# Score maxima turned earlier, norms by a power on GpSimd, one g maximum a slot, in a fused cross-attention and ternary feed-forward block

## The chip, the cores and the metric

The kernel runs on one core of a Trainium2 chip. The metric is the device time of one execution in microseconds; less is better. Times of the kernel before were taken in three runs.

## The reference

The input x is 64 batches of 64 rows of 256, the context is 64 batches of 64 rows of 64. One attention layer with 16 heads and one quantised feed-forward layer are applied, each with a residual.

```python
def attention(hidden_q, kv_c, Wq, w_kc_q, w_kc_kv, W_qr, W_kr, Wo):
    q_big = einsum('bshk,hkq->bshq', (hidden_q @ Wq.T).reshape(b, s, H, K), w_kc_q)
    kv_rope = kv_c * cos + rotate_half(kv_c) * sin
    q_r = einsum('bshq,hqr->bhsr', q_big, W_qr)
    k_r = einsum('bld,hdr->bhlr', kv_rope, W_kr)
    attn = softmax(einsum('bhsr,bhlr->bhsl', q_r, k_r), axis=-1)
    ctx_c = einsum('bhsl,bld->bhsd', attn, kv_rope)
    return einsum('bhsd,hkd->bshk', ctx_c, w_kc_kv).reshape(b, s, H * K) @ Wo.T

def bitlinear158(x, w):
    xn = x / maximum(norm(x), 1e-12) * sqrt(d)
    scale = 127 / clip(max(abs(xn)), 1e-5)          # one scale a row
    xq = clip(round(xn * scale), -128, 127) / scale
    wq = clip(round(w / clip(mean(abs(w)), 1e-5)), -1, 1) * clip(mean(abs(w)), 1e-5)
    return xq @ wq.T

x = x + attention(layernorm(x), ctx, ...)
x = x + bitlinear158(gelu(bitlinear158(layernorm(x), w1)), w2)   # 256 -> 1024 -> 256
```

## The kernel before

The 4096 rows of x make 32 tiles (`NT`) of 128 rows, each two batches. The weights of the attention are folded first: `ah`, `al` (high and low part) take a normed x straight to the queries against the rotated context, `bh`, `bl` take the contexts straight to the output. Each such product is three matmuls in f32r (high by high, low by high, high by low). The first 36 us load and fold; then comes one loop `for n in range(LAST)`, written out in the same form for every engine, that is, five instruction streams which meet only at counting semaphores. An iteration is called **slot n** here. In slot n the engines work on different tiles at once:

- TensorE (PE), in order: `scores(n)`; in even slots `up(n-7)` in both halves (first feed-forward product, bf16); `queries(k, b)`; in odd slots `x_t` (transposes of the next normed x); `project(n-3, 0)` (first half of the output product, 12 matmuls); `turned(n)`, one transpose of `red`, which holds the score maxima of tile n and the exponent sums of tile n-1; `project(n-3, 1)`; `queries(k, b+1)`; in odd slots `up(n-7, 0)`; `shifts(n)` (subtracts the maxima from the scores, in PSUM); `contexts(n-1)`; `down(n-10)` (second feed-forward product); in odd slots `up(n-7, 1)`.
- VectorE (DVE): `quadrant_max(n)` from the scores; `x_max(n-4)`; in even slots `norms`; `row_max(n)` and `row_sum(n-1)` from the transposed `red`; `divide(n-2)` (contexts by the sums); in odd slots `x_lo`; `residual(n-3)`; in odd slots `x_scale`; in even slots `g_max` of two tiles, `g_scale` and `finish` (output with its scale); `quadrant_sum(n)` after the exponential; up to slot 13 the `statistics` of the layer norm of two tiles at the slot's end.
- ScalarE (ACT): gelu, copies out of PSUM, squares, exponentials. Gelu and exponential need different tables, loaded each time (1.28 us).
- GpSimd (POOL): in even slots 4 to 14 `reciprocal_deviations` (four small steps with one power); `x_round`, `g_round` (quantisation, two passes each), `ctx_lo` (low part of the contexts), `centre`, `norm_x`; early on the ternary weights.
- The queue of SP: the transposing transfers `turn_x` (of `xq`) and `turn_g` (of `qb`), `shift_rows(n)` (the row maxima spread over `shift`, which `shifts(n)` reads), `rinv_rows`/`rinv_spread` (reciprocal sums through DRAM to `rb`), `store`.

`norms(j)` makes `scl`, the scales of two x tiles and two g tiles together: a floor, a reciprocal square root by a bit trick and three Newton steps (`rsqrt`, L189 to L201), a product with the maximum and a last floor and factor; 14 instructions of 128x4 elements, each of which waits for the one before. Its semaphore is `norm_steps`; gelu and `finish` wait for it.

`QB` is a pair of PSUM banks that serve queries, transposed x, and `up` in turn (`USES` fixes the order; a use waits until the use two before it has been copied out). So `up(n-7, 0)` of an odd slot waits for `xt_lo` (DVE `x_lo`), and `queries(k, b)` of an even slot waits for the first gelu of that slot. The other bank names: `SB` scores, `CB` contexts, `T` transposed `red`, `O` projection and second product.

Of the kernel before, what the change touches and what calls it, by code (L numbers as in the profile page):

```python
# [24 lines left out]
P = 128  # L25
# [4 lines left out]
F = 1024  # L30
# [16 lines left out]
NEWTON = 3  # L47
RSQRT_OPS = 3 * NEWTON + 2
# [6 lines left out]
NORM_STEPS = RSQRT_OPS + 3  # L55


def build(nc, x, kv, wq, wk_t, wqr, wkr_t, wkv, wo_t, w1_t, w2_t, consts, out):
    with ExitStack() as ctx:
# [32 lines left out]
        least, wfactor = [sb(n, [P, 4], F32) for n in ("least", "wfactor")]  # L92
# [96 lines left out]
        def rsqrt(e, v, y, t, done, n):  # L189

            def step(ins):
                nonlocal n
                n = n + 1
                ins.then_inc(done, 1)
                e.wait_ge(done, n)
            step(e.tensor_scalar(t.bitcast(I32), v.bitcast(I32), 1, None, ALU.arith_shift_right))
            step(e.tensor_scalar(y.bitcast(I32), t.bitcast(I32), -1.0, float(0x5F3759DF), ALU.mult, ALU.add))
            for _ in range(NEWTON):
                step(e.scalar_tensor_tensor(out=t, in0=y, scalar=-0.5, in1=y, op0=ALU.mult, op1=ALU.mult))
                step(e.scalar_tensor_tensor(out=t, in0=t, scalar=1.0, in1=v, op0=ALU.mult, op1=ALU.mult))  # L200
                step(e.scalar_tensor_tensor(out=y, in0=t, scalar=1.5, in1=y, op0=ALU.add, op1=ALU.mult))  # L201
            return n


        def statistics(dve, first, last):

            for t in range(first, last + 1):
                if t < last:
                    if t >= 4:
                        dve.wait_ge(sem["bn_means"], t - 3)  # L210
                    if t % 4 == 0:
                        dve.wait_ge(sem[f"x_loaded{t // 4}"], 16)
                    dve.bn_stats(st6[:, t % 4, :], xs[:, t, :]).then_inc(sem["bn_stats"], 1)
                if t > first:
                    dve.wait_ge(sem["bn_stats"], t)
                    dve.bn_aggr(mv[:, t - 1, :], st6[:, (t - 1) % 4, :]).then_inc(sem["bn_means"], 1)

# [27 lines left out]

        FLOOR1 = EPS_Q * EPS_N * EPS_LN ** 0.5 / D ** 0.5 * D
# [88 lines left out]
        with nc.Block() as block:  # L335
            @block.sync
            def _(sp):
# [98 lines left out]
            def _(pool):  # L436
# [23 lines left out]
                def g_round(t):  # L460
                    pool.wait_ge(sem["g_scale_steps"], 2 * (t // 2 + 1))
# [4 lines left out]
                    pool.tensor_scalar(qb[:, t % 2, :], tq[:, :], 1.0, -MAGIC, ALU.mult, ALU.add).then_inc(sem["g_rounded"], 1)  # L466

# [21 lines left out]
                for k, w in ((0, D), (1, F)):  # L489
                    pool.memset(least[:, 2 * k:2 * k + 2], EPS_N ** 2 * (EPS_LN * D ** 2 if k == 0 else 1.0) / w).then_inc(sem["eps_set"], 1)  # L490
# [12 lines left out]
                for n in range(LAST):  # L503
# [26 lines left out]
            def _(act):  # L530
# [27 lines left out]
                def gelu(t, half):  # L558
                    act.wait_ge(sem["hidden"], 2 * t + half + 1)
                    if half == 0:  # L560
                        act.wait_ge(sem["norm_steps"], NORM_STEPS * (t // 2 + 1))
# [110 lines left out]
            def _(pe):  # L672
# [196 lines left out]
                for n in range(LAST):  # L869
# [3 lines left out]
                    if n % 2 == 0 and tile(n - 7):  # L873
                        up(n - 7, 0)
                        up(n - 7, 1)
                    if k < NB:
                        queries(k, b)
                    if n % 2 and k + 1 < NB:
                        x_t(pe, k + 1)
                    if n == 3:  # L880
                        pe.wait_ge(sem["b_lo_done"], HP // 2)
                    if tile(n - 3):
                        project(n - 3, 0)
                    if n <= NT:
                        turned(n)
                    if tile(n - 3):
# [30 lines left out]
            def _(dve):  # L917
# [59 lines left out]
                def g_scale(p):  # L977
                    c = slice(2 * p, 2 * p + 2)
                    dve.wait_ge(sem["g_maxima"], 2 * p + 2)
                    dve.scalar_tensor_tensor(out=gm[:, c], in0=amax[:, p + 2, 2:4], scalar=FLOOR2, in1=level[:, 2:4], op0=ALU.max, op1=ALU.mult).then_inc(sem["g_scale_steps"], 1)  # L980
                    dve.wait_ge(sem["g_scale_steps"], 2 * p + 1)
                    dve.reciprocal(c2[:, c], gm[:, c]).then_inc(sem["g_scale_steps"], 1)

                def norms(j):

                    c = slice(2 if j >= NB else 0, 2 if j < 2 else 4)
                    v, r, t, m, s = fw[0][:, c], fw[1][:, c], fw[2][:, c], amax[:, j, c], scl[:, j, c]
                    done, n = sem["norm_steps"], NORM_STEPS * j
                    if j < NB:
                        dve.wait_ge(sem["x_squared"], 2 * j + 2)  # L990
                        dve.wait_ge(sem["x_maxima"], 2 * j + 2)
                    if j >= 2:
                        dve.wait_ge(sem["g_squared"], 2 * j - 2)
                        dve.wait_ge(sem["g_maxima"], 2 * j - 2)
                    at_least(dve, done, n)
                    dve.scalar_tensor_tensor(out=v, in0=stat[:, j, c], scalar=1.0, in1=least[:, c], op0=ALU.mult, op1=ALU.max).then_inc(done, 1)
                    dve.wait_ge(done, n + 1)
                    rsqrt(dve, v, r, t, done, n + 1)
# [163 lines left out]
```

## Time and profile before

| | |
|---|---|
| three runs | 455.22, 459.38, 459.72 us; median 459.38 |
| profiled execution | 457.08 us, of which 454.9 are the span from the first instruction to the last |
| mean granted TensorE clock | 0.957 of full speed |
| busy, share of span | PE 86%, DVE 73%, ACT 57%, POOL 56% |

The span and the 2.2 us around it make the profiled execution's 457.08 us. Slot 0 starts at 36.3 us, slot 8 at 122.5, slot 30 at 375.8; the last transposition of `red` is at 400.4 and the last 50 us are the end of the feed-forward part. All durations come from this one execution. PE rows of 128x256 f32 last 0.28 us but start 0.12 us apart, since matmuls overlap.

### The profile page before, as it was taken

The page shows a single profiled execution, that of the slowest core. Times are in us where ns is not written, and L with a number is a line of the kernel's source. Part 1 is how long each engine was busy: PE and PEld are TensorE (multiplying, and loading weights), DVE is VectorE, ACT ScalarE, POOL GpSimd, SP SyncE. Part 2 cuts the span into 40 slices and gives each one's busy share as a digit, 9 for nine tenths or more (in the row PEclk, how much of TensorE's full clock was granted, in tenths as well). Part 3 has the DMA queues.
Part 4 walks back from the last instruction along what each step waited for, and adds up shares of the span by engine and source line. Part 5 has one row for each costly group of instructions (what it writes and reads, how often), then busy time and mean ns, then how long its engine had stood idle before and what let it go on. Part 6 is the DMA issues. An engine that isn't in the chain of part 4 may idle for free.

```text
span 454.9 us, 8971 instructions
## 1 busy us (share of the span) xinstructions
PE 393.1 (86%) x2855; PEld 282.0 (62%) x2870; DVE 330.5 (73%) x873; ACT 257.8 (57%) x477; POOL 255.2 (56%) x321
## 2 busy tenths in 40 slices
PE   9799889794988999989999999999999997876554
PEld 7587557572665776767676767676767674464222
DVE  0364867584798789887878787878787888877564
ACT  1155543332667676675758585858585857556340
POOL 1209447994365656667373738373837373767543
PEclk9899999996999999999999999999999999999665
DMA  8993254443213232424262434252424253443333
GB/s 216 404 333 128 56 142 117 119 117 92 64 52 78 62 79 71 102 48 106 73 107 71 108 73 105 72 107 71 108 72 107 72 107 77 102 127 81 78 97 92
DMA packets 65533, 48.81 MB, mean 107 GB/s; under 512 B 50384, under 2 KB 55888, under 8 KB 65104
## 3 DMA queue, kind: packets, MB, share of 16 engines
q1 hardware_dynamic: 64880, 44.72, 37.8%
q10 hardware_dynamic: 608, 3.54, 2.3%
q8 instruction: 23, 0.38, 0.4%
q14 instruction: 22, 0.18, 0.2%
HBM read 31.98 MB, written 4.46 MB: 80 GB/s over the span
## 4 chain that ended last, share of the span: by engine, by line
POOL 34%; issue 31%; PE 15%; DMA 7%; DVE 6%; SPq 4%; ACT 1%; POOLq 1%; ACTq 0%; DVEq 0%
POOL cl L440 7%; POOL tq L463 6%; POOL qb L466 6%; POOL xa L455 3%; DMA wq_s<-wq 3%; POOL xq L458 3%; POOL yc L450 2%; POOL xn L315 2%; PE hps L786 2%; POOL w_s L478 2%; SPq L365 2%; DMA shift<-nmax 2%; PE ps L744 2%; PE ps L690 2%; DVE cr L953 1%
## 5 line engine op out<-in xcount | busy, mean ns | idle before, releaser
L440 POOL TENSOR_TENSOR cl<-cr,ch 128x512 fp32r<-128x512 f32 x64 | 80.3, 1277 | 131.0 <-ACT ch L550 131.0
L690 PE MATMUL ps<-xh,ah 128*128 128x256 f32 x256 | 75.6, 295 | 4.9 <-ACT g L565 4.5
L754 PE MATMUL hps<-bh,ch 128*128 128x256 f32 x256 | 76.7, 300 | 1.4 <-POOL cl L440 1.4
L534 ACT ACTIVATE qf<-ps 128x512 f32<-128x512 f32 x64 | 37.5, 586 | 65.4 <-PE ps L692 65.4
L755 PE MATMUL hps<-bl,ch 128*128 128x256 f32 x256 | 72.2, 282 | 0.0
L756 PE MATMUL hps<-bh,cl 128*128 128x256 f32 x256 | 72.2, 282 | 0.0
L691 PE MATMUL ps<-xl,ah 128*128 128x256 f32 x256 | 71.9, 281 | 0.0
L692 PE MATMUL ps<-xh,al 128*128 128x256 f32 x256 | 71.8, 280 | 0.0
L550 ACT ACTIVATE ch<-cr 128x512 fp32r<-128x512 f32 x64 | 39.3, 631 | 55.0 <-DVE cr L953 55.0
L690 PEld LDWEIGHTS ps<-xh,ah 128*128 128x128 f32 x256 | 48.2, 188 | 26.7 <-issue 25.8
L786 PE MATMUL hps<-w2q,qt 128*128 128x256 bf16 x256 | 39.1, 303 | 17.3 <-DMA qt<-qb 12.8
L786 PEld LDWEIGHTS hps<-w2q,qt 128*128 128x128 bf16 x256 | 25.0, 107 | 44.7 <-issue 24.4
L930 DVE TRANSPOSE_TENSOR_REDUCE red<-pe 128x16 f32<-128x512 f32 x64 | 41.6, 689 | 14.9 <-ACT pe L545 14.7
L565 ACT ACTIVATE g<-ps,scl 128x512 f32<-128x512 f32 x64 | 41.0, 683 | 19.6 <-PE ps L776 19.4
L923 DVE TRANSPOSE_TENSOR_REDUCE red<-hps 128x16 f32<-128x512 f32 x64 | 41.4, 685 | 12.6 <-PE hps L707 12.3
L754 PEld LDWEIGHTS hps<-bh,ch 128*128 128x128 f32 x256 | 48.4, 189 | 3.2 <-POOL cl L440 1.8
L755 PEld LDWEIGHTS hps<-bl,ch 128*128 128x128 f32 x256 | 48.4, 189 | 0.1
L756 PEld LDWEIGHTS hps<-bh,cl 128*128 128x128 f32 x256 | 48.3, 189 | 0.0
L692 PEld LDWEIGHTS ps<-xh,al 128*128 128x128 f32 x256 | 48.3, 188 | 0.0
L691 PEld LDWEIGHTS ps<-xl,ah 128*128 128x128 f32 x256 | 48.2, 188 | 0.0
L953 DVE TENSOR_TENSOR cr<-ps,rb 128x512 f32<-128x512 f32 x64 | 41.2, 686 | 7.2 <-DMA rb<-rinv_d 4.0
L776 PE MATMUL ps<-w1q,xqt 128*128 128x512 bf16 x113 | 35.1, 403 | 9.5 <-DVE xs L958 5.1
(136 smaller groups left out, 830.2 us busy)
## 6 DMA issues: line engine op xcount, KB each, us to landing
rb<-rinv_d SPq DMA_DIRECT2D x64, 256.0 KB, 3.9
xs<-x SPq DMA_DIRECT2D x8, 512.0 KB, 4.3
out<-yo SPq DMA_DIRECT2D x32, 128.0 KB, 3.5
wq_s<-wq SPq DMA_DIRECT2D x2, 1024.0 KB, 14.4
w_s<-w_t SPq DMA_DIRECT2D x2, 1024.0 KB, 7.2
wo_s<-wo_t ACTq DMA_DIRECT2D x1, 2048.0 KB, 11.1
wk_a<-wk_t SPq DMA_DIRECT2D x2, 512.0 KB, 7.3
kvs<-kvn SPq DMA_DIRECT2D x8, 128.0 KB, 4.1
```

Source lines behind the costliest of these rows:

```text
L440: pool.tensor_tensor(cl[:, u % 2, :, b * S:(b + 1) * S], cr[:, :, b * S:(b + 1) * S], ch[:, u % 2, :, b * S:(b + 1) * S].bitcast(F32), ALU ...
L565: act.activation(g[:, t % GB, 512 * half:512 * half + 512], turn_bank("h", t, half), ACT.Gelu, scale=hscale(scl, t)).then_inc(sem["gelu_do ...
L690: pe.matmul(o, ah[:, c, cols], xh[:, k % 2, c, :], start=(c == 0), stop=False)
L691: pe.matmul(o, ah[:, c, cols], xl[:, k % 2, c, :], start=False, stop=False)
L692: m = pe.matmul(o, al[:, c, cols], xh[:, k % 2, c, :], start=False, stop=(c == KC - 1))
L754: pe.matmul(O[:, 0:D], c_h, bh[:, hp, :], start=(hp == 0), stop=False)
L755: pe.matmul(O[:, 0:D], c_h, bl[:, hp, :], start=False, stop=False)
L756: m = pe.matmul(O[:, 0:D], c_l, bh[:, hp, :], start=False, stop=(hp == HP - 1))
L786: m = pe.matmul(O[:, D:2 * D], qt[:, t % 2, c, :], w2q[:, c, :], start=(c == 0), stop=(c == FC - 1))
L923: dve.tensor_reduce(red[:, u % 2, 16 * b:16 * b + 16], SB[b].rearrange("p (k s) -> p k s", s=32), AX.X, ALU.max, apply_transpose=True).the ...
L930: dve.tensor_reduce(red[:, (u + 1) % 2, 64 + 16 * b:80 + 16 * b], pe32[:, u % 2, b, :].rearrange("p (k s) -> p k s", s=32), AX.X, ALU.add, ...
L953: dve.tensor_tensor(cr[:, :, b * S:(b + 1) * S], CB[b].rearrange("p (h s) -> p h s", s=S), rb[:, b, :].rearrange("p (h s) -> p h s", s=S), ...
```

## The change

1. On PE, `turned(n)` comes before `project(n-3, 0)` in odd slots and in slots without `up`; in even slots with `up`, `project(n-3, 0)` and then `turned(n)` come right after `up`, before `queries(k, b)`.
2. On SP's queue `shift_rows(n)` comes before `turn_g(n-10)` in odd slots.
3. `norms` moves from DVE to POOL, after `x_round` of even slots, and uses the power operation with exponent -0.5 instead of the bit trick and Newton steps: 6 instructions (4 where only one of x and g is there).
4. `g_max` and `g_scale` work on one tile (n-8) in every slot instead of two tiles in even slots; `g_round(t)` waits for its own tile's scale.
5. On DVE, `x_max` comes after `row_sum`; `statistics` comes before `quadrant_sum` and ends in slot 11, with up to three tiles a slot (`STATS`). `reciprocal_deviations` moves to the back of a slot, in slot 4 and in odd slots 7 to 15.

```diff
@@ SP
+                    if tile(n):
+                        shift_rows(n)
                     if n % 2 and tile(n - 10):
                         turn_g(n - 10)
-                    if tile(n):
-                        shift_rows(n)
@@ POOL
+                def norms(j):
+                    halves = [h for h in range(2) if (j < NB, j >= 2)[h]]
+                    c = slice(2 * halves[0], 2 * halves[-1] + 2)
+                    v, r, t = fw
...
+                    for h in halves:
+                        pool.tensor_scalar(v[:, 2 * h:2 * h + 2], stat[:, j, 2 * h:2 * h + 2], (LEAST1, LEAST2)[h], 1.0, ALU.max, ALU.mult).then_inc(done, 1)
+                    n += len(halves)
+                    pool.wait_ge(done, n)
+                    pool.tensor_tensor(r[:, c], v[:, c], mhalf[:, c], ALU.pow).then_inc(done, 1)
+                    pool.wait_ge(done, n + 1)
+                    pool.tensor_tensor(t[:, c], r[:, c], amax[:, j, c], ALU.mult).then_inc(done, 1)
+                    pool.wait_ge(done, n + 2)
+                    for h in halves:
...
+                        pool.tensor_scalar(scl[:, j, 2 * h:2 * h + 2], t[:, 2 * h:2 * h + 2], EPS_Q, wfactor[:, 2 * h:2 * h + 1], ALU.max, ALU.mult).then_inc(done, 1)
...
-                    if n % 2 == 0 and 4 <= n < 16:
-                        reciprocal_deviations(pool, n // 2)
                     if n % 2 == 0 and tile(n - 6):
                         x_round(n - 6)
                         x_round(n - 5)
+                    if n % 2 == 0 and 0 <= (n - 6) // 2 < NB + 2:
+                        norms((n - 6) // 2)
...
+                    if n == 4 or n % 2 and 7 <= n < 16:
+                        reciprocal_deviations(pool, n // 2)
@@ PE
                     if n % 2 == 0 and tile(n - 7):
                         up(n - 7, 0)
                         up(n - 7, 1)
+                        if tile(n - 3):
+                            project(n - 3, 0)
+                        if n <= NT:
+                            turned(n)
                     if k < NB:
                         queries(k, b)
                     if n % 2 and k + 1 < NB:
                         x_t(pe, k + 1)
+                    if (n % 2 or not tile(n - 7)) and n <= NT:
+                        turned(n)
...
                     if tile(n - 3):
-                        project(n - 3, 0)
-                    if n <= NT:
-                        turned(n)
-                    if tile(n - 3):
+                        if n % 2 or not tile(n - 7):
+                            project(n - 3, 0)
                         project(n - 3, 1)
@@ DVE
-                    if tile(n - 4):
-                        x_max(n - 4)
-                    if n % 2 == 0 and 0 <= (n - 6) // 2 < NB + 2:
-                        norms((n - 6) // 2)
                     if tile(n):
                         row_max(n)
                     if tile(n - 1):
                         row_sum(n - 1)
+                    if tile(n - 4):
+                        x_max(n - 4)
...
-                    if n % 2 == 0 and tile(n - 8):
+                    if tile(n - 8):
                         g_max(n - 8)
-                        g_max(n - 7)
-                        g_scale((n - 8) // 2)
-                        if tile(n - 10):
+                        g_scale(n - 8)
+                        if n % 2 == 0 and tile(n - 10):
                             finish(n - 10)
...
+                    if 2 <= n < 12:
+                        statistics(dve, STATS[n - 2], STATS[n - 1])
```

PE in an even slot (slot 24), from `up` on. `w1q` is the first feed-forward product, `xh`/`xl` with `ah`/`al` the queries, `bh`/`bl` with `ch`/`cl` the projection, `ident` with `red` the transposition `turned`. Before:

```order
L776 MATMUL ps1<-w1q_57,xqt_105 128x512 [waits gelu_done,xqt_turned1]
L776 MATMUL ps1<-w1q_57,xqt_105 128x512
L690 MATMUL ps0<-xh_87,ah_50 128x256 [waits gelu_done,xt_lo]
L691 MATMUL ps0<-xl_88,ah_50 128x256
L692 MATMUL ps0<-xh_87,al_51 128x256
...
L754 MATMUL hps1<-bh_52,ch_94 128x256 [waits residuals,outputs,ctx_lo]
L755 MATMUL hps1<-bl_53,ch_94 128x256
L756 MATMUL hps1<-bh_52,cl_95 128x256
...
L721 MATMUL hps1<-ident_55,red_91 128x128 [waits row_maxima,rinv_steps,quad_sums,quad_maxima]
L754 MATMUL hps1<-bh_52,ch_94 128x256
```

Now:

```order
L790 MATMUL ps1<-w1q_57,xqt_104 128x512 [waits gelu_done,xqt_turned1]
L790 MATMUL ps1<-w1q_57,xqt_104 128x512
L768 MATMUL hps1<-bh_52,ch_93 128x256 [waits residuals,outputs,ctx_lo]
L769 MATMUL hps1<-bl_53,ch_93 128x256
L770 MATMUL hps1<-bh_52,cl_94 128x256
...
L735 MATMUL hps1<-ident_55,red_90 128x128 [waits row_maxima,rinv_steps,quad_sums,quad_maxima]
L704 MATMUL ps0<-xh_86,ah_50 128x256 [waits gelu_done,xt_lo]
L705 MATMUL ps0<-xl_87,ah_50 128x256
L706 MATMUL ps0<-xh_86,al_51 128x256
```

The twelve matmuls of the first half projection and the transposition have moved ahead of the twelve of the queries, the ones that wait for gelu.

DVE in an even slot (slot 12), from `quadrant_max` on. Before (the nine Newton instructions are cut to the first three):

```order
L923 TENSOR_REDUCE red_91<-hps0 128x16 [waits scores]
L963 TENSOR_REDUCE amax_74<-yc_98 128x1 [waits x_centred]
L996 SCALAR_TENSOR_TENSOR fw0_68<-stat_73,least_76 128x4 [waits g_maxima,g_squared,norm_steps,x_maxima,x_squared]
L199 SCALAR_TENSOR_TENSOR fw2_70<-fw1_69 128x4 [waits norm_steps]
L200 SCALAR_TENSOR_TENSOR fw2_70<-fw2_70,fw0_68 128x4 [waits norm_steps]
L201 SCALAR_TENSOR_TENSOR fw1_69<-fw2_70,fw1_69 128x4 [waits norm_steps]
...
L1001 SCALAR_TENSOR_TENSOR scl_75<-fw2_70,wfactor_77 128x4 [waits norm_steps]
L936 TENSOR_REDUCE nmax_102<-hps1 32x64 [waits shift_rows0,red_turned]
L942 TENSOR_REDUCE rs_103<-hps1 32x64 [waits red_turned]
```

Now:

```order
L941 TENSOR_REDUCE red_90<-hps0 128x16 [waits scores]
L954 TENSOR_REDUCE nmax_101<-hps1 32x64 [waits shift_rows0,red_turned]
L960 TENSOR_REDUCE rs_102<-hps1 32x64 [waits red_turned]
L964 RECIPROCAL ri_103<-rs_102 32x64 [waits rinv_stored1,rinv_steps]
L981 TENSOR_REDUCE amax_74<-yc_97 128x1 [waits x_centred]
```

The row maxima follow the quadrant maxima at once; the norms are gone to POOL and the x maximum stands behind the reciprocal.

The queue of SP in an odd slot (slot 23), from the store of the slot before. Before:

```order
L374 DMA out<-yo_106 128x256 [waits outputs]
L370 DMA_TRANSPOSE qt_110<-qb_109 128x8x128 [waits products,g_rounded]
L343 DMA shift_90<-nmax_102 2x16x32 [waits shifted,row_maxima]
L343 DMA shift_90<-nmax_102 2x16x32
L370 DMA_TRANSPOSE qt_110<-qb_109 128x8x128 [waits products,g_rounded]
```

Now:

```order
L362 DMA out<-yo_105 128x256 [waits outputs]
L331 DMA shift_89<-nmax_101 2x16x32 [waits shifted,row_maxima]
L331 DMA shift_89<-nmax_101 2x16x32
L358 DMA_TRANSPOSE qt_109<-qb_108 128x8x128 [waits products,g_rounded] x2
L339 DMA rinv_d<-ri_103 16x2x32 [waits rinv_spread,rinv_steps]
```

The transposing transfer of tile n-10 now stands behind the wait for the row maxima.

## Rows read from the trace of the kernel before

**Rows 1.** The page, part 1: busy us, share of the span and instructions by engine.

```profile
PE 393.1 (86%) x2855; PEld 282.0 (62%) x2870; DVE 330.5 (73%) x873; ACT 257.8 (57%) x477; POOL 255.2 (56%) x321
```

**Rows 2.** Waits: engine, line, releaser: us in total, times, longest us.

```profile
PE hps L734 <- DMA shift<-nmax: 15.2, 10, 6.4
...
POOL tq L463 <- DVE c L982: 10.9, 3, 5.3
...
PE ps L776 <- DVE xs L958: 5.1, 8, 0.6
PE ps L690 <- ACT g L565: 4.5, 11, 0.4
...
PE ps L776 <- DVE xl L332: 1.9, 3, 0.6
```

**Rows 3.** Timeline of PE, slots 23 and 24: start us, us, line, idle before.

```profile
299.72 0.36 PE L754 MATMUL hps<-bh,ch 128*128 128x256 f32 x1
...
303.95 0.28 PE L691 MATMUL ps<-xl,ah 128*128 128x256 f32 x1
304.07 0.28 PE L692 MATMUL ps<-xh,al 128*128 128x256 f32 x1
304.99 0.38 PE L776 MATMUL ps<-w1q,xqt 128*128 128x512 bf16 x1 [0.64 <-DVE xs L958]
...
310.69 0.36 PE L690 MATMUL ps<-xh,ah 128*128 128x256 f32 x1 [0.44 <-ACT g L565]
...
313.62 0.27 PE L721 MATMUL hps<-ident,red 128*128 128x128 f32 x1
...
316.80 0.73 PE L734 MATMUL hps<-shift,em 128*128 128x512 f32 x2
```

**Rows 4.** Timeline of DVE, slots 23 and 24.

```profile
298.55 1.27 DVE L923 TRANSPOSE_TENSOR_REDUCE red<-hps 128x16 f32<-128x512 f32 x2
...
304.88 0.58 DVE L969 SCALAR_TENSOR_TENSOR gm<-amax,level 128x2 f32<-128x2 f32 x1
...
310.88 0.15 DVE L996 SCALAR_TENSOR_TENSOR fw<-stat,least 128x4 f32<-128x4 f32 x1
...
313.93 0.28 DVE L936 TENSOR_REDUCE nmax<-hps 32x64 fp32r<-32x128 f32 x1 [0.33 <-PE hps L721]
```

**Rows 5.** Timeline of POOL, end of slot 24.

```profile
316.58 2.52 POOL L440 TENSOR_TENSOR cl<-cr,ch 128x512 fp32r<-128x512 f32 x2 [7.35 <-ACT ch L550]
```

**Rows 6.** Groups by line: busy us, mean ns of one, idle before.

```profile
L226 POOL TENSOR_TENSOR rstd<-nw,mhalf 128x4 f32<-128x4 f32 x8 | 8.1, 1016 | 0.0
```

**Rows 7.** Timeline of SP's queue, slot 23.

```profile
299.81 2.07 SPq L370 DMA_TRANSPOSE qt<-qb  x1
301.98 1.40 SPq L343 DMA_DIRECT2D shift<-nmax  x2
```

**Rows 8.** Timeline of POOL, SP's queue and PE, slot 6.

```profile
99.76 0.20 POOL L223 TENSOR_SCALAR nw<-mv 128x4 f32<-128x4 f32 x1
...
101.52 0.49 POOL L455 TENSOR_SCALAR xa<-yc,c 128x256 f32<-128x256 f32 x1
...
105.24 1.82 SPq L343 DMA_DIRECT2D shift<-nmax  x2
...
108.27 1.22 PE L734 MATMUL hps<-shift,em 128*128 128x512 f32 x2 [6.37 <-DMA shift<-nmax]
```

**Rows 9.** Stretches of slot 6 and slots 22-23: us, busy PE, PEld, DVE, ACT, POOL, clock, DMA.

```profile
285.10:308.20 23.10, 21.96 (x168) 16.24 (x168) 18.13 (x48) 15.95 (x30) 13.08 (x16) 1.00 0.39 88
...
106.00:108.00 2.00, 0.00 (x0) 0.00 (x0) 0.00 (x0) 0.07 (x1) 2.00 (x3) 0.50 0.05 8
```

**Rows 10.** Timeline of PE and DVE, slot 30.

```profile
379.12 0.27 PE L721 MATMUL hps<-ident,red 128*128 128x128 f32 x1
...
381.13 0.28 DVE L936 TENSOR_REDUCE nmax<-hps 32x64 fp32r<-32x128 f32 x1
...
384.00 0.72 PE L734 MATMUL hps<-shift,em 128*128 128x512 f32 x2 [3.17 <-DMA shift<-nmax]
```

More of the change, by code:

```diff
@@ L54, with norm_count @@
 LAST = NT + 10
-NORM_STEPS = RSQRT_OPS + 3
+def norm_count(j):
+    return sum(6 if 2 <= i < NB else 4 for i in range(j + 1))
 def build(nc, x, kv, wq, wk_t, wqr, wkr_t, wkv, wo_t, w1_t, w2_t, consts, out):
@@ L91, in build @@
         stat, amax, scl = [sb(n, [P, NB + 2, 4], F32) for n in ("stat", "amax", "scl")]
-        least, wfactor = [sb(n, [P, 4], F32) for n in ("least", "wfactor")]
+        wfactor = sb("wfactor", [P, 4], F32)
         level = sb("level", [P, 4], F32)
@@ L187, in at_least @@
                 e.wait_ge(s, value)
[L189 to L202, printed above, removed]
         def statistics(dve, first, last):
@@ L216, in statistics @@
                     dve.bn_aggr(mv[:, t - 1, :], st6[:, (t - 1) % 4, :]).then_inc(sem["bn_means"], 1)
+        STATS = (8, 10, 12, 15, 18, 21, 24, 26, 28, 30, 32)
         def reciprocal_deviations(pool, part):
@@ L244, in rope @@
             return e.tensor_tensor(kvn[:, c, :], kvn[:, c, :], r, ALU.add)
+        LEAST1, LEAST2 = EPS_N ** 2 * EPS_LN * D, EPS_N ** 2 / F
         FLOOR1 = EPS_Q * EPS_N * EPS_LN ** 0.5 / D ** 0.5 * D
@@ L460, in g_round @@
                 def g_round(t):
[L461 removed]
+                    pool.wait_ge(sem["g_scale_steps"], 2 * (t + 1))
                     at_least(pool, sem["g_rounded"], t)
@@ L466, in g_round @@
                     pool.tensor_scalar(qb[:, t % 2, :], tq[:, :], 1.0, -MAGIC, ALU.mult, ALU.add).then_inc(sem["g_rounded"], 1)
+                def norms(j):
+                    halves = [h for h in range(2) if (j < NB, j >= 2)[h]]
+                    c = slice(2 * halves[0], 2 * halves[-1] + 2)
+                    v, r, t = fw
+                    done, n = sem["norm_steps"], norm_count(j - 1)
+                    if j < NB:
+                        pool.wait_ge(sem["x_squared"], 2 * j + 2)
+                        pool.wait_ge(sem["x_maxima"], 2 * j + 2)
+                    if j >= 2:
+                        pool.wait_ge(sem["g_squared"], 2 * j - 2)
+                        pool.wait_ge(sem["g_maxima"], 2 * j - 2)
+                    at_least(pool, done, n)
+                    for h in halves:
[7 more added lines that the diff above has]
+                    for h in halves:
+                        if j in (0, 2):
+                            pool.wait_ge(sem["w_mean_steps"], 4 * h + 4)
+                        pool.tensor_scalar(scl[:, j, 2 * h:2 * h + 2], t[:, 2 * h:2 * h + 2], EPS_Q, wfactor[:, 2 * h:2 * h + 1], ALU.max, ALU.mult).then_inc(done, 1)
                 def ternary_1():
@@ L984, in norms @@
[L984 to L998, printed above, removed]
-                    dve.scalar_tensor_tensor(out=t, in0=r, scalar=1.0, in1=m, op0=ALU.mult, op1=ALU.mult).then_inc(done, 1)
-                    dve.wait_ge(done, n + NORM_STEPS - 1)
-                    dve.scalar_tensor_tensor(out=s, in0=t, scalar=EPS_Q, in1=wfactor[:, c], op0=ALU.max, op1=ALU.mult).then_inc(done, 1)
@@ L1003, in finish, with g_scale @@
+                def g_scale(t):
+                    c = slice(t, t + 1)
+                    dve.wait_ge(sem["g_maxima"], t + 1)
+                    dve.scalar_tensor_tensor(out=gm[:, c], in0=gscale(amax, t), scalar=FLOOR2, in1=level[:, 2:3], op0=ALU.max, op1=ALU.mult).then_inc(sem["g_scale_steps"], 1)
+                    dve.wait_ge(sem["g_scale_steps"], 2 * t + 1)
+                    dve.reciprocal(c2[:, c], gm[:, c]).then_inc(sem["g_scale_steps"], 1)
                 def finish(t):
                     dve.wait_ge(sem["products"], t + 1)
-                    dve.wait_ge(sem["norm_steps"], NORM_STEPS * (t // 2 + 3))
+                    dve.wait_ge(sem["norm_steps"], norm_count(t // 2 + 2))
```

13 lines of the change are left out of this document (1 added, 12 removed).

## The prediction, made before the changed kernel had run

> **What bounds the kernel now.** The page first [rows 1]: PE is busy for 393 of 454.9 us, no other engine for over 331. PE alone is near its limit, so what its instruction stream waits for is what there is to win. The waits come next [rows 2]; I take those of PE and leave out the long ones of POOL and ACT, which have idle time to spare. PE waits 15.2 us in ten places for the shift rows, 4.5 us in eleven places for a gelu before queries, and 5.1 + 1.9 = 7.0 us in eleven places for DVE before `up`. Together that is 26.7 us. The timeline tells where they stand [rows 3]: once a pair of slots, in slots 8 to 29 (eleven pairs), 0.64 us before `up(n-7, 0)` of the odd slot (304.99) and 0.44 before the queries of the even one (310.69; 0.29 in the first two pairs). Matmuls of 128x256 start 0.12 us apart and are shown 0.28 long, so a gap shown behind one is really 0.16 longer: PE could have started at 304.19. Of the ten shift waits 6.37 us are slot 6 [rows 8], 3.17 slot 30 [rows 10], and the longest of the rest is near 1 us.
>
> **The change, part by part.**
>
> Even slots. The 12 projection matmuls of tile n-3 need its `ctx_lo`, which was made a slot before (the one at 316.58 serves slot 25 [rows 5]), so they fill the time in which gelu runs: 12 x 0.12 = 1.4 us against a wait of 0.44. That wait goes: 2 x 0.29 + 9 x 0.44 = 4.5 us, the whole row. The transposition, at 313.62, came after 24 matmuls; now 12 and no wait stand before it, so it comes about 0.44 + 1.43 = 1.9 us sooner, at 311.7. It needs the quadrant maxima, which come from the scores and end near 310.7, so it waits for nothing. The row maxima then follow. Before, the norms started at 310.88 and ended near 313.6 on DVE [rows 4]: left there they would hold the maxima up, so the early transposition is worth nothing without the move to POOL. Rows on their way take 316.80 - 314.24 = 2.6 us from issue; issued at 312.4 they land at 315.0, when PE is still in the projection. The shift waits of the even slots from 8 to 16 go: 15.2 - 6.37 - 3.17, less about 1.0 in slot 31 and 0.9 in slots 1 and 2, leaves 3.8 us.
>
> Odd slots. `up(n-7, 0)` waited for `x_lo` on DVE, behind row maxima that came at the projection's half. With the transposition 12 matmuls (1.43 us) sooner, the whole chain of DVE (row maxima, sums, reciprocal, division, `x_lo`) comes up to 1.4 us sooner, less 0.38 for the x maximum which now stands inside it: about 1.0 sooner against the true gap of 0.8. The 7.0 us go. The price: the quadrant maxima end at 298.55 + 1.27 = 299.82 [rows 4], and PE reaches this place at 299.72 [rows 3], so the transposition now waits 0.13 us with its semaphore, eleven times 0.13 = 1.4 us, and nothing hides it any more.
>
> The sum for slots 8 to 29: 4.5 + 7.0 + 3.8 - 1.4 = 13.9 us, and 0.16 for each of some sixteen gaps behind 128x256 matmuls, 2.6 us: 16.5.
>
> The norms on POOL. The four steps of `reciprocal_deviations` take 101.52 - 99.76 = 1.76 us with a power of 1.02 us [rows 6, 8]; norms have two short instructions more, so 2.3 us against 2.7 on DVE. In the even slots they lie in POOL's idle 7.35 us before `ctx_lo` [rows 5]. That is their cover, and they cost nothing there. Bounds: 0, and if the cover were gone 2.3 x 11 = 25 us. I take 0, since 5 us of cover remain. Gelu needs them a slot later, and their inputs (squares, maxima) are made in the slot before.
>
> One g maximum a slot. The maxima and scales of a tile are some 1.2 + 0.35 us of DVE. They leave the even slot and enter the odd one, where DVE had waits of 0.6, 0.3 and 1.0 us (behind `x_scale` at 304.88 + 0.58 [rows 4]) and its chain is now 1.0 us ahead. I cost this at nothing; bound 0.5 us a pair, 5 us, if the scores' maxima get late. The small scale instruction at 304.88, issued while POOL worked at `ctx_lo`, took 0.58 us; one of the same size as the norms' first took 0.15 at 310.88 with POOL idle [rows 4]. What stands beside POOL's long instructions can thus cost 0.43 us more, and this is where the 0.5 us a pair of that bound comes from.
>
> A rule of the Trainium skill speaks against this part: "SBUF: two separate sides" of SBUF — State Buffer says that a VectorE instruction with two operands from SBUF and a GpSimd instruction lock each other out of a port they share, for the whole length of the one that came first. The trace agrees at 304.88. By it both the moved norms and the second scale of a pair put more such meetings into the odd slot; at one meeting more a pair the sum would be 4.7 us smaller, by my own count none.
>
> SP's queue. In odd slots `turn_g(n-10)` was issued at 299.81 and took 2.07 us, so the shift rows went at 301.98 [rows 7]. Row maxima ready at 300.2 would have waited behind it; now they go first, and `turn_g` is issued near 301.9, its data needed by `down` near 306. Bounds: 0, and 0.5 us a pair if transposing transfers take over 4 us to land. I take 0.
>
> Slots 0 to 7. In slot 6 POOL did the reciprocal deviations before `x_round`, then SP sent two transposes, then the shift rows at 105.24, which PE met at 108.27 after 6.37 us [rows 8]. The deviations now come a slot later, so everything there is 1.76 us sooner; the norms of 4 us on DVE leave that slot too, but the rows stay behind the transposes. The early transposition also takes away the waits of 0.66 (shift, slot 2), 0.42 and 0.69 (division, waiting for the spread sums) and 0.71 (normed x behind POOL's ternary weights, whose start moves with slot 3): 2.5 us. (These four are single gaps of PE in its timeline; of them only the slot 6 rows are shown.) Together 4.3; bounds 1.8 and 6.5.
>
> Slot 30 and the end. PE's transposition at 379.12 ends at 379.39, the row maxima start at 381.13 since DVE is at the norms [rows 10]: 1.7 us of the 3.17 go. In the end DVE's maxima and norms stand before the g scale that POOL waits for, up to 5.3 us [rows 2]. But the last tile's rounding on POOL comes after the last norms (2.3 us), which need the last squares, so I give the end 1 us only; bounds -1 and +5. Together 2.7.
>
> Sum: 16.5 + 4.3 + 2.7 = 23.5, and 457.1 - 23.5 = 433.6 us on the profiled execution's own scale. That one is 2.3 below the median of the three runs, which lie 4.5 apart; I add 1 and say **435 us**. With the bounds on both sides the likeliest case reaches from 428 to 441.
>
> **The rivals.**
>
> (a) The queues give half back. SP's transposes, now behind the shift rows, and DVE's fuller odd slot turn into new waits of `down`, of the transposition or of the first `up`, 0.5 us a slot in 22 slots, 11 us: 446. For it: PE has an in-order stream, a wait removed in one place tends to be met at the next. Against: margins of over 1 us at each place that I worked out.
>
> (b) The clock helps too. At 106 to 108 us the granted clock was 0.50, that is 1.2 GHz, while PE stood in slot 6 [rows 9], and the work after it ran at that until near 112. If the shorter wait does not bring it on there and in slot 30, some 1.8 + 1.7 us of work come back (the work at half speed in either place, halved), and if the end gives 5 us rather than 1, that makes 7.5: 427. The Trainium skill ("What's actually happening", TensorE: Matmul & The Clock Gate) says that an inactive TensorE gets the low clock and activity gives the high one back; the trace agrees, as the clock fell there after PE had been idle.
>
> (c) Slower than before. The transposition in odd slots and in slots without `up` now has no projection ahead of it, so PE stands still for whatever DVE is late with the quadrant maxima. Before, it had 1.43 us of cover. DVE's odd slot gets 1.6 us more. If DVE becomes the bound, each of 22 slots takes what DVE takes: it is busy 18.1 of 23.1 us in a pair [rows 9], of which the norms' 2.7 leave. From 2.2 us a pair on, 24 us, it eats the whole gain; at 3 us a pair the time is 466. For that DVE would have to grow by over 7 us a pair, so it is unlikely.
>
> (d) No change. The waits are given back wholly, since the modelled ends of matmuls hide that PE is at its limit: 456 to 459. Against it stands the rate within a slot: matmuls start 0.12 us apart when nothing waits, and did not start in the gaps.
>
> **How the numbers follow.** Forecast 0.63, (a) 0.16, (b) 0.12, (c) 0.04, (d) 0.05. The range takes in the forecast's bounds and all but the edges of (a) and (b): 426 to 447. Faster by over 1% is the forecast, (a) and (b): 0.91; within 1% (d), 0.05; slower (c), 0.04. About 1% is what a measurement of this kernel can tell from no change, as its three runs lie 1% apart.
>
> **What would show it.** Right: no wait of PE for gelu before queries and none for DVE before `up` in odd slots; row maxima 1.5 to 2 us sooner after the scores; a pair of slots at 21.5 us instead of 22.7 to 23.1 [rows 9]; the wait of slot 6 at 4 to 5 us; POOL's norms at 2.3 us inside a wait for ACT. Wrong: PE waiting for quadrant maxima over 0.3 us a slot, `down` waiting for `qt` in the middle of the run, or pairs still at 22.5 us or more.

## The result, and the profile after

The changed kernel takes 434.12 us (median of 4 runs, 433.48 to 437.54), the kernel before 458.54 (4 runs, 455.22 to 459.72). The medians lie 24.4 us apart; the ratio is 0.9491, with a 95% interval of 0.9429 to 0.9553. (Ratios, here and below, come from undisturbed runs set beside runs of the kernel before on the same chip, and so differ a little from the quotient of the medians.) The forecast was 435.

The profiled execution took 437.54 us, with a span of 435.7, and is the longest of the four; the spans of the others are 431.7 to 432.7. The difference lies ahead of the first slot: loading takes until 39.15 us in it, and took until 36.34 in the profiled execution before. In all profiles of this study that point lies between 36.2 and 40.4 us, whichever kernel runs, so I compare stretches that begin at PE's first scores of a slot; the last one ends with the issue of the last store:

| stretch, us | before | after | difference | predicted |
|---|---|---|---|---|
| up to slot 0 | 36.34 | 39.15 | +2.8 | 0 |
| slots 0 to 7 | 86.19 | 84.22 | -2.0 | -4.3 |
| slots 8 to 29 | 253.27 | 235.86 | -17.4 | -16.5 |
| slot 30 to the last store | 77.32 | 74.67 | -2.65 | -2.7 |

The three stretches behind the load gain 22.1 us together, where the forecast had 23.5.

**The page**, part 1 (answers [rows 1]): busy us, share of the span and instructions.

```profile
PE 385.8 (89%) x2870; PEld 279.5 (64%) x2870; DVE 308.4 (71%) x653; ACT 258.2 (59%) x477; POOL 292.1 (67%) x419
```

DVE has lost 220 instructions and 22 us, POOL has gained 98 and 37 us. Neither number is the gain: PE is still the busiest engine, and what went is its idle time.

**The waits** (answers [rows 2]): engine, line, releaser, us in total, times, longest us.

```profile
DVE nmax L954 <- PE hps L735: 25.1, 32, 2.4
...
PE hps L800 <- DMA qt<-qb: 19.2, 7, 5.1
...
PE hps L748 <- DMA shift<-nmax: 7.9, 6, 4.8
...
PE hps L735 <- DVE red L941: 4.3, 5, 2.0
```

The two rows of PE waiting for `x_scale` or `x_lo` ahead of `up`, and that for gelu ahead of queries, are gone; the shift rows are down from 15.2 to 7.9 us, of which 4.8 is slot 6 and 1.61 slot 30. The last row is the new wait, for the quadrant maxima ahead of the transposition. 2.02 of its 4.3 us are in slot 31 and 1.16 in slots 1 and 3, where 0.94 was there before; in slots 8 to 29 it shows in two places, with 0.78 us in slot 11 and 0.35 in slot 29. `down` now waits 19.2 us in seven places for its transposed input (`qt`), where it waited 12.8 in four; all of them are in slot 31 and behind it.

**Timeline of PE**, a pair in the steady part (answers [rows 3]): start us, us, line.

```profile
286.48 0.60 PE L315 MATMUL ps<-ident,xn 128*128 128x128 f32 x4
286.99 0.33 PE L735 MATMUL hps<-ident,red 128*128 128x128 f32 x1
287.09 0.36 PE L768 MATMUL hps<-bh,ch 128*128 128x256 f32 x1
...
291.28 0.28 PE L706 MATMUL ps<-xh,al 128*128 128x256 f32 x1
291.40 0.60 PE L790 MATMUL ps<-w1q,xqt 128*128 128x512 bf16 x2
...
294.83 1.09 PE L721 MATMUL hps<-qf,kvt 64*64 64x512 f32 x8
295.85 1.04 PE L790 MATMUL ps<-w1q,xqt 128*128 128x512 bf16 x4
296.54 0.47 PE L768 MATMUL hps<-bh,ch 128*128 128x256 f32 x1
...
298.12 0.27 PE L735 MATMUL hps<-ident,red 128*128 128x128 f32 x1
298.14 0.36 PE L704 MATMUL ps<-xh,ah 128*128 128x256 f32 x1
...
302.35 0.28 PE L706 MATMUL ps<-xh,al 128*128 128x256 f32 x1
302.47 0.62 PE L748 MATMUL hps<-shift,em 128*128 128x512 f32 x2
```

No row of the whole pair has a bracket with an idle time. `up` at 291.40 starts 0.12 us behind the matmul ahead of it, queries at 298.14 right behind the transposition, and the shift matmuls at 302.47 start 0.12 behind the last of the queries: PE runs at its own rate. In the odd slot the transposition (286.99) stands ahead of the whole projection, in the even one (298.12) behind its first half.

**Timeline of DVE**, the same pair (answers [rows 4]).

```profile
285.66 1.27 DVE L941 TRANSPOSE_TENSOR_REDUCE red<-hps 128x16 f32<-128x512 f32 x2
...
293.11 0.34 DVE L998 SCALAR_TENSOR_TENSOR gm<-amax,level 128x1 f32<-128x1 f32 x1
...
295.99 1.31 DVE L941 TRANSPOSE_TENSOR_REDUCE red<-hps 128x16 f32<-128x512 f32 x2 [0.74 <-PE hps L721]
298.42 0.28 DVE L954 TENSOR_REDUCE nmax<-hps 32x64 fp32r<-32x128 f32 x1 [1.12 <-PE hps L735]
...
302.88 1.12 DVE L998 SCALAR_TENSOR_TENSOR gm<-amax,level 128x1 f32<-128x1 f32 x1
```

In the odd slot the quadrant maxima end at 285.66 + 1.27 = 286.93 and the transposition starts at 286.99: it follows them, as predicted, and the page calls it no wait since the four transposes of normed x (286.48) are still modelled as running. It starts 0.51 us behind the first of these; in slot 7, where the maxima had long been done (115.95), the same distance is 116.46 - 116.03 = 0.43. So the wait is near 0.1 us. In the even slot the maxima end at 297.30, 0.8 us before PE gets to the transposition. The row maxima come 298.42 - 294.83 = 3.6 us after the scores' first matmul; before it was 313.93 - 308.19 = 5.7, from the same slot's scores in the kernel before:

```profile
308.19 1.09 PE L707 MATMUL hps<-qf,kvt 64*64 64x512 f32 x8
```

**Timeline of POOL**, the norms in the even slot (answers [rows 5, 6]).

```profile
295.50 0.52 POOL L470 TENSOR_SCALAR fw<-stat 128x2 f32<-128x2 f32 x2
296.11 1.02 POOL L473 TENSOR_TENSOR fw<-fw,mhalf 128x4 f32<-128x4 f32 x1
...
297.52 0.59 POOL L480 TENSOR_SCALAR scl<-fw,wfactor 128x2 f32<-128x2 f32 x2
302.70 2.50 POOL L428 TENSOR_TENSOR cl<-cr,ch 128x512 fp32r<-128x512 f32 x2 [4.60 <-ACT ch L564]
```

The norms take 298.11 - 295.50 = 2.6 us and 4.60 us of idle time are left behind them. **Stretch** of the pair (answers [rows 9], where PE was busy 21.96 of 23.10 us):

```profile
284.00:305.00 21.00, 21.00 (x163) 15.55 (x162) 17.45 (x35) 15.49 (x28) 14.89 (x22) 1.00 0.40 95
```

**Slots 6, 30 and 31** (answers [rows 8, 10]), from the timelines of SP's queue and then of PE.

```profile
103.14 2.59 SPq L353 DMA_TRANSPOSE xqt<-xq  x2
105.84 1.83 SPq L331 DMA_DIRECT2D shift<-nmax  x2
...
372.24 1.36 SPq L331 DMA_DIRECT2D shift<-nmax  x2
373.70 2.66 SPq L358 DMA_TRANSPOSE qt<-qb  x2
```

```profile
108.88 1.22 PE L748 MATMUL hps<-shift,em 128*128 128x512 f32 x2 [4.79 <-DMA shift<-nmax]
...
365.80 0.73 PE L748 MATMUL hps<-shift,em 128*128 128x512 f32 x2 [1.61 <-DMA shift<-nmax]
371.56 0.33 PE L735 MATMUL hps<-ident,red 128*128 128x128 f32 x1 [2.02 <-DVE red L941]
...
378.91 1.05 PE L800 MATMUL hps<-w2q,qt 128*128 128x256 bf16 x8 [2.34 <-DMA qt<-qb]
```

Slot 6: the row maxima are ready at 99.8 (DVE's row starts at 99.51 and takes 0.28), the shift rows leave at 105.84, since they are still behind two transposes that wait for POOL. Slots 30 and 31: the shift wait is half of what it was, and two others have come: 2.02 us for the quadrant maxima, and 2.34 of `down` for a `turn_g` that now goes behind the shift rows, at 373.70. In slot 31 PE has no queries and no transposes of x left between the scores and the transposition, so nothing covers the wait for the maxima.

### The profile page after: what moved, and what is told of

Read it like the earlier page. It is cut to its first block and busy times, and to the rows that moved or that the text cites. A ratio compares the mean times of both kernels' runs of the same rounds, so it can differ in the third digit from the quotient of the medians.

```text
span 435.7 us, 8866 instructions
## 1 busy us (share of the span) xinstructions
PE 385.8 (89%) x2870; PEld 279.5 (64%) x2870; DVE 308.4 (71%) x653; ACT 258.2 (59%) x477; POOL 292.1 (67%) x419
## 3 DMA queue, kind: packets, MB, share of 16 engines
q10 hardware_dynamic: 608, 3.54, 2.4%
## 5 line engine op out<-in xcount | busy, mean ns | idle before, releaser
L768 PE MATMUL hps<-bh,ch 128*128 128x256 f32 x256 | 75.7, 296 | 1.4 <-POOL cl L428 1.4
L800 PE MATMUL hps<-w2q,qt 128*128 128x256 bf16 x256 | 36.3, 289 | 19.8 <-DMA qt<-qb 19.2
L564 ACT ACTIVATE ch<-cr 128x512 fp32r<-128x512 f32 x64 | 38.3, 627 | 24.9 <-DVE cr L971 24.9
L800 PEld LDWEIGHTS hps<-w2q,qt 128*128 128x128 bf16 x256 | 23.9, 103 | 45.4 <-DMA qt<-qb 23.4
L941 DVE TRANSPOSE_TENSOR_REDUCE red<-hps 128x16 f32<-128x512 f32 x64 | 41.4, 686 | 13.9 <-PE hps L721 13.9
L993 DVE TENSOR_REDUCE amax<-g 128x1 f32<-128x1024 f32 x32 | 38.7, 1209 | 2.0 <-ACT g L579 2.0
```

What stands on the lines that cost most here:

```text
L768: pe.matmul(O[:, 0:D], c_h, bh[:, hp, :], start=(hp == 0), stop=False)
L800: m = pe.matmul(O[:, D:2 * D], qt[:, t % 2, c, :], w2q[:, c, :], start=(c == 0), stop=(c == FC - 1))
L941: dve.tensor_reduce(red[:, u % 2, 16 * b:16 * b + 16], SB[b].rearrange("p (k s) -> p k s", s=32), AX.X, ALU.max, apply_transpose=True).the ...
```

## The experiments

In these kernels each of the two transposing transfers (`turn_x`, `turn_g`) is replaced by two plain copies of its halves on the same queue, so the feed-forward activations arrive untransposed and the output is not the reference's; the waits for these transfers count both copies, and everything else is computed as before. I call this the copy form. Two runs say what it does by itself. The edit of `turn_g`, shortened; that of `turn_x` is alike:

```diff
-sp.dma_start_transpose(qt[:, t % 2, :, :], qb[:, t % 2, :]).then_inc(sem[f"gqt_turned{t % 2}"], 16)
+for c in range(2):
+    sp.dma_start(qt[:, t % 2, 4 * c:4 * c + 4, :], qb[:, t % 2, 512 * c:512 * c + 512]...).then_inc(sem[f"gqt_turned{t % 2}"], 16)
```

**The kernel before in copy form.** Expected: 

> The kernel before, with each transposing transfer (of xq and of qb) replaced by two plain copies of its halves on the same queue; the quantised activations reach the feed-forward products untransposed, so this part of the computation is not the reference's. It is the base for kernels of the same form. My theory: the queue takes about as long (two issues of 0.6 us against one of 1.24) and landing is 3 to 4 us against 2.8, which only the end feels: 457 to 463. Rival, that transposing transfers were what the shift rows waited for: under 452.

Measured: 457.14 us (10 runs, 454.17 to 458.76) beside 455.78 for the kernel before; ratio 1.0021, interval 0.9992 to 1.005. The copies landed 2.1 to 2.2 us after their issue (medians), not the 3 to 4 that I expected.

**The changed kernel in copy form.** Expected: 

> The changed kernel with the same replacement (feed-forward activations untransposed). If the gain does not hang on the transposing transfers, the ratio to the copy form of the kernel before is again near 0.95: 433 to 439, 22 to 25 us under it. Rival, that part of the gain came from shift rows no longer standing behind slow transposing transfers: a gain of under 18 us in this form.

Measured: 433.28 us (4 runs, 429.54 to 437.49), ratio 0.9473, interval 0.9401 to 0.9545, where the change itself gave 0.9491. The profiled execution is the longest of the four, with a load until 40.39 us, so again the stretches are compared: its slots 8 to 29 take 234.68 us (235.86 with transposes), those of the kernel before in copy form 252.43 (253.27). The copy form keeps the times of both kernels, so what is undone in it can be read against it. This run also shows that the gain doesn't need the time that a transposing transfer takes.

**The old order on PE.** The changed kernel, with PE's stream alone put back.

```diff
                         up(n - 7, 1)
-                        if tile(n - 3):
-                            project(n - 3, 0)
-                        if n <= NT:
-                            turned(n)
...
-                    if (n % 2 or not tile(n - 7)) and n <= NT:
-                        turned(n)
...
                     if tile(n - 3):
-                        if n % 2 or not tile(n - 7):
-                            project(n - 3, 0)
+                        project(n - 3, 0)
+                    if n <= NT:
+                        turned(n)
+                    if tile(n - 3):
                         project(n - 3, 1)
```

Expected: 

> Copy form of the changed kernel (feed-forward activations untransposed) with the old order on PE alone; norms on POOL, one g maximum a slot, the shift rows ahead of turn_g and the moved statistics stay. Base 433.3; the copy form of the kernel before is at 457.1. My theory: the waits for gelu before queries and for DVE before the first up return, in full, 12 to 14 us, and the row maxima come 1.4 to 1.9 us later again: 448 to 452, so the order on PE is worth 15 to 19 of the 24 us and the rest 5 to 9. Rival, that the norms taken off DVE are the larger part and the order adds little: under 440.

Measured: 453.54 us (12 runs, 450.99 to 455.18), ratio 0.9967, interval 0.9937 to 0.9997, that is 0.1 to 2.9 us less than the kernel before, and a longer time than I expected. So with the old order the rest of the change (norms on POOL, shift rows first, one g maximum a slot, x maximum and statistics moved) is worth 1.5 us against the kernel before, and some 2.5 against its copy form (0.9967 / 1.0021 = 0.9946), with about 2 us of uncertainty. The order, put onto the rest, is worth some 20: 20.3 between the medians, 22 by the two ratios (0.9967 - 0.9473; the two runs were on different chips), and 253.91 - 234.68 = 19.2 in slots 8 to 29. The waits of PE and of the row maxima say why:

```profile
DVE nmax L952 <- PE hps L737: 64.4, 32, 3.7
...
PE ps L792 <- DVE xl L320: 10.2, 11, 1.0
...
PE hps L750 <- DMA shift<-nmax: 8.8, 7, 4.3
...
PE ps L706 <- ACT g L581: 4.5, 11, 0.4
```

DVE is free earlier, but uses it to wait 64.4 us for PE's transposition, where it waits 25.1 with the new order. The wait for gelu is the same 4.5 us in the same eleven places as in [rows 2], and that for DVE before `up` is longer, 10.2 instead of 7.0 us, with the x maximum inside DVE's chain now. And yet the shift rows are in time: in slots 8 to 29 PE waits 0.16 us for them, where it was 3.8. The rest of the change does win those 3.7 us without the order, and gives 3.2 of them back before `up`; slots 8 to 29 take 253.91 us, with 253.27 before. What is left of it is from slot 30 on, 73.60 us against 77.32; 2.0 of that is slot 30, where the norms no longer stand ahead of DVE's row maxima and the shift wait is 2.2 instead of 3.2 us. So what was taken off DVE is not the cause by itself: without the order it is lost again at the next fixed place. Whether the order would do it without the rest was not tried.

**Slot 6: the shift rows ahead of the transposes.** The trace of after says that the rows stand behind `turn_x`, which waits for POOL.

```diff
                 for n in range(LAST + 1):
+                    if n == 6:
+                        shift_rows(n)
                     if n % 2 == 0 and tile(n - 6):
                         turn_x(n - 6)
                         turn_x(n - 5)
-                    if tile(n):
+                    if tile(n) and n != 6:
                         shift_rows(n)
```

Expected: 

> Copy form of the changed kernel with one more change: in slot 6 SP sends the shift rows ahead of the transfers of xq. Base 433.3. PE waits 4.8 us there, since the rows stand behind a wait for x rounding, which stands behind the ternary weights on POOL. My theory: the row maxima are ready 6 us sooner, the whole wait goes, and with it the low clock behind it: 5 to 7 us less, 426 to 429. Rival, that POOL's late work takes over the wait in slot 7 (ctx_lo, normed x): 431 or more.

Measured: 433.48 us (6 runs, 431.56 to 434.59), ratio 0.9485, interval 0.9441 to 0.9528: no less than without the edit. My expectation fell. The rival's time held, but its reason only in part: normed x from POOL is 0.93 us of the new waits, and the largest has another cause. Slots 6 and 7 took 26.63 us, against 26.90 in the copy form of the changed kernel. SP's queue, DVE and PE, slots 6 and 7:

```profile
98.23 1.41 SPq L331 DMA_DIRECT2D shift<-nmax  x2
101.56 2.91 SPq L354 DMA_DIRECT2D xqt<-xq  x4
104.51 0.59 SPq L377 DMA_DIRECT2D xs<-x  x1
105.22 0.83 SPq L339 DMA_DIRECT2D rinv_d<-ri  x2
109.99 1.31 SPq L348 DMA_DIRECT2D rb<-rinv_d  x2
```

```profile
98.55 0.55 DVE L968 RECIPROCAL ri<-rs 32x64 f32<-32x64 f32 x1
...
114.95 1.29 DVE L975 TENSOR_TENSOR cr<-ps,rb 128x512 f32<-128x512 f32 x2 [3.94 <-issue]
116.16 0.68 DVE L320 TENSOR_TENSOR xl<-ps,xh 128x512 fp32r<-128x512 f32 x1
```

```profile
108.58 0.66 PE L315 MATMUL ps<-ident,xn 128*128 128x128 f32 x4 [0.93 <-POOL xn L303]
...
116.99 1.01 PE L794 MATMUL ps<-w1q,xqt 128*128 128x512 bf16 x2 [3.54 <-DVE xl L320]
```

The edit did what it should: the rows leave at 98.23, right behind the row maxima, and the wait of 4.6 us is gone. But the reciprocals of the slot, ready at 99.10, have also to pass the transfers that wait for POOL's rounding. They leave at 105.22, behind a load of 512 KB of x (104.51); the queue waits 3.9 us for them to land (the median in the kernel before is 1.4), spreads them from an issue at 109.99, and the division starts at 114.95; `x_lo` is behind it on DVE, and PE waits 3.54 us for that before `up` of slot 7, 0.93 for normed x and 0.53 for the scores' exponentials. There were two things behind the transposes, and the one that I let past was only the first to be missed. That the reciprocals are what holds slot 7 is read from these rows; moving them too was not tried, nor moving the load of x. The waits of PE in slots 6 and 7 add up to 5.6 us here and to 5.1 in the copy form without the edit.

**Slot 6, slots 30 to 31 and the end together.** To the edit above it adds the old queue order from slot 30 on, the transposition of slot 30 ahead of the projection, and POOL's last g roundings ahead of the norms.

```diff
+                    if n >= 30 and n % 2 and tile(n - 10):
+                        turn_g(n - 10)
                     if tile(n) and n != 6:
                         shift_rows(n)
-                    if n % 2 and tile(n - 10):
+                    if n < 30 and n % 2 and tile(n - 10):
                         turn_g(n - 10)
...
+                    if n % 2 == 0 and n >= 32 and tile(n - 9):
+                        g_round(n - 9)
...
+                        if n == 30:
+                            turned(n)
```

Expected: 

> Copy form of the changed kernel with the slot 6 change and three more: from slot 30 on turn_g again ahead of the shift rows; in slot 30 the transposition ahead of the projection; from slot 32 on, in even slots, g rounding on POOL ahead of norms, contexts and centring. My theory: 6 us of slot 6, 2 of down in slot 31, 0.8 in slot 30, 3 at the end, as the transfer of the rounded g goes about 2.6 us sooner: 421 to 424. Rival, that at the end norms and centring moved back cost what the rounding gains: 425 to 427.

Measured: 425.76 us (6 runs, 424.94 to 428.89), ratio 0.9341, interval 0.93 to 0.9382: 7.7 us less than the run above, taken on the same chip in turns with it, and the fastest of the study. It lies where the rival put it, 425 to 427. But my 421 to 424 had 6 us for slot 6 in it, which the run above does not have; for the other three places I had 5.8. In the profiles 5.3 us are from slot 30 to the last store (68.80 against 74.05), and 2.7 are in slots 0 to 29, where the two programs are the same: so much is not the edits'. PE's largest wait in it:

```profile
PE hps L808 <- DMA qt<-qb: 9.3, 5, 3.1
```

`down` waits 9.3 us for `qt`, where it waited 17.0 without the three edits. In the end of the changed kernel POOL does the norms first, from 399.21 to 401.82, then both g roundings, and `turn_g` goes at 404.65 with `down` 5.07 us late; in this kernel the first rounding stands ahead of the norms (from 392.17, norms from 394.40) and that `down` waits for nothing above 1.8 us. How the 5.3 us divide between the three edits was not tried, nor whether this version gains with the transposing transfers.

Not tried at all: PE's new order alone on the kernel before (so it stays open how much of the gain would be there without the offloading), the norms on POOL alone or back on DVE, the queue order, the g maxima or the statistics back one by one.

## Why the prediction was right

**Where the time was.** The time came from PE's waits in slots 8 to 29, as the forecast said: 17.4 us against 16.5. That the total, 434.12 for 435, fits so much better than the parts is luck: the medians lie 24.4 us apart and the stretches 22.1, and the runs of one kernel differ by 4 us. PE's waits in the rows of slots 8 to 29 fell from 15.7 to 3.4 us, by 12.3, where I had 13.9 (0.64 of my 7.0 before `up` stands in slot 7, at 120.20). The other 5.1 us stand in no row; I had put 2.6 behind the modelled ends of matmuls, counting sixteen gaps. The eleven ahead of the queries follow matmuls that start 0.22 us apart and are shown 0.38 long, and would add 1.8 by the same reckoning. From slot 12 to 27 a pair takes 20.96 to 21.53 us where it took 22.6 to 24.0, but the last one, slots 28 and 29, gained nothing (21.78, before 21.87): 0.57 us of waiting for the shift rows, issued at 343.23 behind two transposes, and 0.35 for the maxima are new there. In the copy form the first of them is missing and the pair takes 20.95. PE is busy for the whole of a pair, so rival (d), that nothing could be won behind modelled ends, is out.

**Even slots.** The wait for gelu ahead of the queries is gone, and the row maxima come 2.1 us sooner after the scores (predicted 1.9). The run with PE's old order has the wait back at its full 4.5 us, so PE's order is what covers it: shown.

**Odd slots.** The wait for `x_lo` is gone, and is back (10.2 us) with the old order: shown too. The price, 0.13 us a pair, is right in place (transposition at 286.99, maxima at 286.93), and near 0.1 in size. It shows nowhere as a row of its own in this pair, as transposes of normed x are ahead of it; where it does show in slots 8 to 29 it is 1.1 us in two places, against a predicted 1.4 in all. New as well are the 0.57 us of slot 28 and 0.60 in slot 9, for the exponentials.

**Norms on POOL.** 2.6 us, predicted 2.3; hidden, with 4.6 us of idle time left, as predicted. The prediction also said that the transposition is worth nothing without them. The runs don't show that, as norms on DVE with the new order weren't tried; what they show is the other half: norms on POOL, with all the other moves, are worth 1.5 to 2.5 us without the order, and that the steady shift waits go with these moves and not with the order, to which the forecast gave a share of them.

**One g maximum a slot.** Cost nothing that shows, as predicted, though the size at its bound was too small: the small scale takes 1.12 us in the even slot, beside POOL's `ctx_lo` (from 302.70), and 0.34 in the odd one, where I had 0.58 and 0.15 from [rows 4]. All 32 together are

```profile
L998 DVE SCALAR_TENSOR_TENSOR gm<-amax,level 128x1 f32<-128x1 f32 x32 | 22.5, 703 | 1.1
```

against 3.0 us (16 of 186 ns) before. "SBUF: two separate sides" (SBUF — State Buffer) of the Trainium skill has a VectorE instruction with two inputs from SBUF and a GpSimd instruction that reads SBUF lock each other out for the whole of the one that came first, and by it most of the 1.12 would be a wait for the end of a `ctx_lo`; the trace agrees, as the first of the two that take 2.50 us from 302.70 ends near 303.95 and the scale at 304.00. No run here takes POOL's instruction away. It costs no time here, because DVE still waits 0.94 us for `down` behind it (at 305.13).

**Slots 0 to 7: the step that failed.** "The early transposition also takes away the waits of 0.66, 0.42, 0.69 and 0.71: 2.5 us." Of 4.3 us for these slots 2.0 came, just inside the lower bound. These 2.5 us were not won at all: in slots 0 to 2 no tile is at its projection yet, so the transposition had nothing to be moved ahead of, and 0.56 of the 0.66 and 0.36 of the 0.42 stay. The wait for normed x grew from 0.71 to 1.32, and only the 0.69 went down, to 0.23; the four are still 2.5 us together. Slot 6 gave 6.37 - 4.79 = 1.6 (predicted 1.76), but behind it PE worked longer at half clock: 3.8 us at 0.50 before, 5.6 now, which makes the scores of slot 7 take 1.93 us instead of 1.08. What made up for that is the 0.64 us ahead of `up` in slot 7. The run with the rows first shows that sending them earlier still gives no more. The work behind the wait of slot 6, before and after:

```profile
108.30:112.10 3.80, 3.80 (x18) 1.96 (x22) 2.15 (x6) 1.68 (x3) 0.81 (x2) 0.50 0.42 132
...
108.90:114.50 5.60, 5.60 (x22) 2.15 (x22) 1.30 (x2) 1.68 (x3) 1.18 (x3) 0.50 0.44 144
```

**Slot 30 and the end.** 2.65 against 2.7, but by other terms than I gave: slot 30 alone gained 12.13 - 9.23 = 2.9 (1.56 of it the shift wait, the rest the clock, as shown below), and from slot 31 on nothing came, as the 2.02 and 2.34 us of new waits there stand against whatever the end won; I had put the end at 1. Rival (a), the queue behind the shift rows and the uncovered transposition, is therefore real in this one place; in the 22 slots where it would have cost 11 us PE waits 1.1 us for the transposition.

**The clock**, rival (b), which the forecast left out of its sum: it failed in slot 6 and held in slot 30. In slot 6 after the wait the granted clock is 0.50 (1.2 GHz) again, so the shorter wait didn't keep it up. In slot 30 it did: before, PE worked at 0.50 behind the wait of 3.17 us, and after the wait of 1.61 it stays at 1.00. Half of 2.70 us is 1.35, which with the 1.56 of the wait makes the 2.9 of this slot. Before and after, columns as in [rows 9]:

```profile
385.20:387.90 2.70, 2.70 (x16) 1.04 (x8) 1.35 (x3) 1.40 (x4) 2.67 (x3) 0.50 0.61 161
...
359.20:368.40 9.20, 7.59 (x56) 4.77 (x55) 7.33 (x14) 7.52 (x14) 5.47 (x10) 1.00 0.38 95
```

## What to carry to other kernels

A row of short waits of the engine that bounds a kernel is best read as an order: for each, look for work of that engine whose inputs are long there, and put it between. Freeing the engine that is waited for gives little if that engine then waits for the bound one: here everything but the order gave 1.5 to 2.5 us, and the order some 20 on top of it. And where a transfer is let past another in an in-order queue, list everything else behind that one: here the next thing in it was the next to be missed.

## What the runs showed of the hardware

With the rows first in slot 6 the granted clock stayed at 1.00 from 98 to 116 us, and yet the two slots took as long as in the run where PE stood and then worked at half clock. The half clock had only moved: behind the new wait of 3.54 us (up to 116.99) PE worked at 0.50 until 123.1.

```profile
98.00:116.00 18.00, 13.84 (x111) 11.48 (x111) 9.55 (x24) 5.92 (x14) 9.79 (x17) 1.00 0.37 97
...
117.00:123.10 6.10, 6.10 (x22) 1.50 (x22) 3.36 (x12) 4.13 (x6) 5.51 (x11) 0.50 0.34 86
```

In the run with all edits, whose program is the same up to slot 30, a wait of 3.38 us at the same place was followed by 3.4 us at 0.50 and not by 6.1, so a part of what two profiles differ by is the clock's.

The load phase took 36.2 to 40.4 us in the profiled executions, with the same instructions in it in all these kernels, which is about as much as the runs of one kernel lie apart. Its length goes with the granted clock from 18 to 32 us (which of the two brings the other isn't shown): 36.2 us at a mean of 1.00, 36.3 to 37.6 at 0.88, 37.5 at 0.76, and 39.2 and 40.4 at 0.63. The shortest load (the kernel before in copy form) and that of the changed kernel:

```profile
18.00:32.00 14.00, 12.20 (x112) 9.22 (x112) 7.95 (x23) 5.76 (x11) 3.75 (x8) 1.00 1.03 386
...
18.00:32.00 14.00, 12.08 (x71) 8.39 (x72) 5.02 (x11) 3.90 (x7) 3.75 (x8) 0.63 0.78 278
```

So the 2.8 us in the first row of the table need not be the change's: the last two kernels, which contain it, loaded in 36.8 and 37.6 us. Whether the load is the cause of the runs' spread isn't shown, as each kernel has one profile.
